# Expert rows of a mixture-of-experts layer padded to 128 instead of 256, with two blocks of separate experts in a slot

## What is computed

```python
def _L0_ffn_ref(x, Wg, bg, W1, b1, W2, b2):      # 4096 rows, D 256, FF 1024, 8 experts, top 2
    gate_logits = xt @ Wg + bg
    gate_scores = jax.nn.softmax(gate_logits, axis=-1)
    topk_scores, topk_idx = jax.lax.top_k(gate_scores, TOP_K)
    topk_scores = topk_scores / jnp.sum(topk_scores, axis=-1, keepdims=True)
    combine = jnp.sum(jax.nn.one_hot(topk_idx, N_EXPERTS, dtype=xt.dtype) * topk_scores[..., None], axis=1)
    h = jax.nn.gelu(jnp.einsum('td,edf->etf', xt, W1) + b1[:, None, :], approximate=False)
    expert_out = jnp.einsum('etf,efd->etd', h, W2) + b2[:, None, :]
    out = jnp.einsum('te,etd->td', combine, expert_out)
...
x = x + _L0_gnn_ref(_layernorm(x, axis=-1), adj, L0_gnn_W, L0_gnn_b)
x = x + _L0_ffn_ref(_layernorm(x, axis=-1)[None], L0_ffn_Wg, ...)[0]
x = x + _L1_gnn_ref(_layernorm(x, axis=-1), adj, L1_gnn_W, L1_gnn_b)
x = x + _L1_ffn_ref(_layernorm(x, axis=-1)[None])[0]
```

## Time and profile before

| | |
|---|---|
| median of three runs | 1059.9 us (1057.33 to 1060.02) |
| span of the profiled execution | 1056.5 us |
| TensorE busy | 954.7 us (90%), 6711 matmuls |
| VectorE, ScalarE, GpSimd busy | 539.1, 403.2 and 359.3 us |
| first-layer matmuls of the experts | 1776, 201.6 us |
| second-layer matmuls of the experts | 1776, 199.9 us |
| gelu on ScalarE | 296, 124.0 us |
| gathers and scatters on GpSimd | 72 and 74, 71.6 and 122.2 us |

### The profile page before, as it was taken

How to read it: one execution, slowest core, us unless ns; L and a number is a source line. 1 busy time by engine, 2 the same in 40 slices (tenths; PEclk the granted TensorE clock), 3 DMA queues, 4 the chain that set the end, 5 groups by cost and what they waited for, 6 DMA issues and landing times. The chain is left out here.

```text
span 1056.5 us, 22251 instructions
## 1 busy us (share of the span) xinstructions
PE 954.7 (90%) x6711; PEld 625.2 (59%) x6712; DVE 539.1 (51%) x1602; ACT 403.2 (38%) x820; POOL 359.3 (34%) x414
## 2 busy tenths in 40 slices
PE   4988999999923899999999999999839999999994
PEld 1444544444511689889898888889714454444542
DVE  6744212218499665655656566565536333150644
ACT  4862767666787423233232323323102101010111
POOL 3410000014567244545455454554535320110110
PEclk9999999999965899999999999999969999999998
DMA  9885898899788432323323233232359978875781
GB/s 338 326 290 174 286 334 323 295 349 361 277 292 230 143 63 41 56 45 48 53 43 53 45 50 50 42 54 45 55 173 394 409 265 298 293 241 187 227 277 40
DMA packets 92079, 199.84 MB, mean 189 GB/s; under 512 B 14368, under 2 KB 47904, under 8 KB 91904
## 3 DMA queue, kind: packets, MB, share of 16 engines
q1 hardware_dynamic: 70304, 164.17, 44.4%
q0 software_dynamic: 17552, 30.88, 14.7%
q10 hardware_dynamic: 4176, 4.19, 1.2%
HBM read 176.54 MB, written 22.68 MB: 189 GB/s over the span
## 5 line engine op out<-in xcount | busy, mean ns | idle before, releaser
L962 PE MATMUL bank<-adj_f,feat 128*128 128x512 f16 x1024 | 241.2, 391 | 16.6 <-DMA adj_f<-in_adjT 14.9
L1230 ACT ACTIVATE act_f<-bank,b_sb 128x256 f32<-128x256 f32 x296 | 124.0, 470 | 275.5 <-PE bank L1167 275.5
L1167 PE MATMUL bank<-rT,experts 128*128 128x256 f16 x1776 | 201.6, 274 | 3.0 <-DVE rT L1255 3.0
L1179 PE MATMUL bank<-experts,act_h 128*128 x1776 | 199.9, 273 | 0.0
L1167 PEld LDWEIGHTS bank<-rT,experts 128*128 x1776 | 174.1, 98 | 24.6 <-issue 3.4
L1179 PEld LDWEIGHTS bank<-experts,act_h 128*128 128x128 f16 x1776 | 172.0, 98 | 19.5
L962 PEld LDWEIGHTS bank<-adj_f,feat 128*128 128x128 f16 x1024 | 97.7, 97 | 143.7 <-issue 18.7
L1611 PE MATMUL bank<-adj_g,feat 128*128 128x512 f16 x768 | 179.6, 387 | 0.7 <-POOL feat L1437 0.7
L846 ACT ACTIVATE spent<-adj_f 128x1024 f16<-128x1024 f32 x128 | 135.1, 1055 | 33.6 <-DMA adj_f<-in_adjT 28.3
L1097 POOL DMA_INDIRECT x_rows<-y,token x74 | 122.2, 1651 | 65.5 <-issue 56.9
L1611 PEld LDWEIGHTS bank<-adj_g,feat 128*128 128x128 f16 x768 | 73.8, 96 | 94.4 <-issue 1.2
(11 more groups left out here) (259 smaller groups left out, 930.1 us busy)
## 6 DMA issues: line engine op xcount, KB each, us to landing
adj_f<-in_adjT SPq DMA_DIRECT2D x128, 512.0 KB, 6.5
adj_g<-in_adjT SPq DMA_DIRECT2D x72, 512.0 KB, 6.0
adj_early<-in_adjT SPq DMA_DIRECT2D x24, 512.0 KB, 7.1
adj_g<-in_adjT SPq DMA_DIRECT2D x48, 256.0 KB, 3.2
unit_f<-in_W SPq DMA_DIRECT2D x16, 512.0 KB, 7.4
stage<-in_W SPq DMA_DIRECT2D x12, 512.0 KB, 6.4
x_ring<-in_x POOLq DMA_DIRECT2D x16, 256.0 KB, 7.2
x_rows<-agg SPq DMA_DIRECT2D x4, 1024.0 KB, 8.5
```

Of the source, the lines that this page charges most:

```text
L962: last = pe.matmul(mine(s)[ib * DC + c][:, :], feat0[:, j, h, c * P:(c + 1) * P], adj_0[j % RING][:, ib * HALF_SWEEP:(ib + 1) * HALF_SWEEP ...
L1167: last = pe.matmul(pb[2 + q][:, k * SLOT:(k + 1) * SLOT], w1_part(e * DC + (f // FQ * W2_UNIT0 + c), wh)[:, (f % FQ) * P:(f % FQ + 1) * P] ...
L1179: last = pe.matmul(pb[6 + r][:, 0:D], act_h[:, ah, f, r * P:(r + 1) * P], experts[:, ds(e * DC + (W2_UNIT0 + f // UH), 1), wh, (f % UH) * ...
L1230: last = a.activation(act_f[q][:, k, :], pb[2 + q][:, k * SLOT:(k + 1) * SLOT], ACT.Gelu, bias=b1_sb[:, ds(e * FC + (2 * q + k), 1)], scal ...
```

## The change

The rows of an expert are rounded up to 128. A slot is still 256 places, but these are two blocks of 128 that may belong to two experts, and `table` holds an expert number for each block (`TABLE` = 76 entries in place of 40). All that depends on the expert is done per block: TensorE's weights in the first layer (so its matmuls have 128 moving columns, 96 a slot) and in the second, gelu and its bias on ScalarE (4 instructions of 128 columns a quarter), the gate copy and the second bias on VectorE. `BLOCKS` goes from 80 to 72. The compare table `past` moves from PSUM into the space of `row_hot` in SBUF.

```diff
-MAX_SLOTS = (2 * T + E * (SLOT - 1)) // SLOT
-MAX_PAIRS = (MAX_SLOTS + 1) // 2
-BLOCKS = 2 * MAX_PAIRS * SR
+MAX_BLOCKS = (2 * T + E * (P - 1)) // P
+MAX_SLOTS = (MAX_BLOCKS + SR - 1) // SR
+BLOCKS = MAX_SLOTS * SR
+TABLE = BLOCKS + 2 * SR
...
-    past = pb[6][:, P:P + 2 * MAX_PAIRS * E].rearrange("p (s e) -> p s e", e=E)
+    past = row_hots[:, :, :, :].rearrange("p i q c -> p (i q c)")[:, 0:TABLE * E].rearrange("p (s e) -> p s e", e=E)
...
-            st.link(v.tensor_scalar(need_i, running[:, NT, :], float(SLOT - 1), None, ALU.add))
-            st.link(v.tensor_single_scalar(need_i, need_i, -SLOT, ALU.bitwise_and))
+            st.link(v.tensor_scalar(need_i, running[:, NT, :], float(P - 1), None, ALU.add))
+            st.link(v.tensor_single_scalar(need_i, need_i, -P, ALU.bitwise_and))
...
-            def expert_of(s):
-                return pe.value_load(table[0:1, ds(s, 1)], min_val=0, max_val=E - 1)
+            def experts_of(s):
+                return [pe.value_load(table[0:1, ds(s * SR + r, 1)], min_val=0, max_val=E - 1) for r in range(SR)]
...
                     f = 2 * q + k
-                    m = 0
-                    for c in range(DC):
-                        for wh, xh in ((0, 0), (0, 1), (1, 0)):
-                            last = pe.matmul(pb[2 + q][:, k * SLOT:(k + 1) * SLOT],
-                                             w1_part(e * DC + (f // FQ * W2_UNIT0 + c), wh)[:, (f % FQ) * P:(f % FQ + 1) * P],
-                                             rT[:, xh, c, :], start=(m == 0), stop=(m == 5))
-                            m += 1
+                    for r in range(SR):
+                        m = 0
+                        for c in range(DC):
+                            for wh, xh in ((0, 0), (0, 1), (1, 0)):
+                                last = pe.matmul(pb[2 + q][:, k * SLOT + r * P:k * SLOT + (r + 1) * P],
+                                                 w1_part(e[r] * DC + (f // FQ * W2_UNIT0 + c), wh)[:, (f % FQ) * P:(f % FQ + 1) * P],
+                                                 rT[:, xh, c, r * P:(r + 1) * P], start=(m == 0), stop=(m == 5))
+                                m += 1
...
                             last = pe.matmul(pb[6 + r][:, 0:D], act_h[:, ah, f, r * P:(r + 1) * P],
-                                             experts[:, ds(e * DC + (W2_UNIT0 + f // UH), 1), wh,
+                                             experts[:, ds(e[r] * DC + (W2_UNIT0 + f // UH), 1), wh,
...
-                e = a.value_load(table[0:1, ds(s, 1)], min_val=0, max_val=E - 1)
+                e = [a.value_load(table[0:1, ds(s * SR + r, 1)], min_val=0, max_val=E - 1) for r in range(SR)]
...
-                        last = a.activation(act_f[q][:, k, :], pb[2 + q][:, k * SLOT:(k + 1) * SLOT], ACT.Gelu,
-                                            bias=b1_sb[:, ds(e * FC + (2 * q + k), 1)], scale=1.0 / WS)
+                        for r in range(SR):
+                            last = a.activation(act_f[q][:, k, r * P:(r + 1) * P], pb[2 + q][:, k * SLOT + r * P:k * SLOT + (r + 1) * P],
+                                                ACT.Gelu, bias=b1_sb[:, ds(e[r] * FC + (2 * q + k), 1)], scale=1.0 / WS)
...
-                v.tensor_copy(gates[:, ds(s * SR, SR)], rows[:, :, ds(D + e, 1)].rearrange("p r a -> p (r a)")
-                              ).then_inc(sem("gates_taken"), 1)
+                for r in range(SR):
+                    last = v.tensor_copy(gates[:, ds(s * SR + r, 1)], rows[:, r, ds(D + e[r], 1)])
+                last.then_inc(sem("gates_taken"), 1)
...
-                                                  in1=b2_all[:, ds(e, 1), :].rearrange("p a d -> p (a d)"),
+                                                  in1=b2_all[:, ds(e[r], 1), :].rearrange("p a d -> p (a d)"),
```

More of the change, by code:

```diff
@@ L45 @@
 MIDDLE_RING = 4
-LAST_SLOT = 2 * MAX_PAIRS
+LAST_SLOT = TABLE
 ROW = D + E
@@ L117, in program @@
     spare = keep("spare", [P, 1], F32)
-    slots_i = keep("slots_i", [P, 2 * MAX_PAIRS], I32)
+    slots_i = keep("slots_i", [P, TABLE], I32)
     dg = keep("dg", [P, NT], F32)
@@ L133, in program @@
     tokens = keep("tokens", [P, BLOCKS + 4 * SR], I32)
-    gates = keep("gates", [P, BLOCKS], F32)
+    gates = keep("gates", [P, TABLE], F32)
     shift1 = gates[:, 0:NT]
-    table = keep("table", [P, 64], I32)
+    table = keep("table", [P, TABLE + 4], I32)
     grow = keep("grow", [P, P], F32)
@@ L240, in program @@
     w = Region(SUM_AT, SUMS_END)
-    row_hot = [w(f"row_hot{i}", [P, HOTS, P], F16) for i in range(2)]
+    row_hots = w("row_hots", [P, 2, HOTS, P], F16)
+    row_hot = [row_hots[:, i, :, :] for i in range(2)]
     blk_hot = [w(f"blk_hot{i}", [P, HOTS, BLOCKS], F16) for i in range(2)]
@@ L271, in program @@
     need = pb[7][:, (at := next(small)):at + E]
-    slots_f = pb[7][:, (at := next(small)):at + 2 * MAX_PAIRS]
+    slots_f = pb[7][:, (at := next(small)):at + TABLE]
     w1_v = w1_flat.rearrange("p (h a t) f -> p a t h f", h=2, t=2)
@@ L818, in _ @@
             st.link(v.tensor_copy(slots_f, slots_i[:, :]))
-            st.link(v.tensor_tensor(past, slots_f.unsqueeze(2).broadcast_to([P, 2 * MAX_PAIRS, E]),
-                                    end_at[:, :].unsqueeze(1).broadcast_to([P, 2 * MAX_PAIRS, E]), ALU.is_ge))
+            st.link(v.tensor_tensor(past, slots_f.unsqueeze(2).broadcast_to([P, TABLE, E]),
+                                    end_at[:, :].unsqueeze(1).broadcast_to([P, TABLE, E]), ALU.is_ge))
             st.link(v.tensor_reduce(slots_f, past, AX, ALU.add))
-            st.did(v.tensor_scalar(table[:, 0:2 * MAX_PAIRS], slots_f, float(E - 1), None, ALU.min))
+            st.did(v.tensor_scalar(table[:, 0:TABLE], slots_f, float(E - 1), None, ALU.min))
             st.link(v.tensor_scalar(table[:, LAST_SLOT:LAST_SLOT + 1], end_at[:, E - 1:E], -1.0, None, ALU.add))
@@ L1064, in _ @@
                 i, m = q // HOTS % 2, q % HOTS
-                pe.matmul(pb[2][:, 0:BLOCKS], row_hot[i][:, m, :], blk_hot[i][:, m, :], start=(q == 0), stop=(q == 2 * NT - 1)
+                pe.matmul(pb[2][:, 0:BLOCKS], row_hots[:, i, m, :], blk_hot[i][:, m, :], start=(q == 0), stop=(q == 2 * NT - 1)
                           ).then_inc(sem("inverse_used"), 1)
@@ L1192, in _ @@
             keep_busy(pe, pb[1], 8)
-            e = expert_of(0)
+            e = experts_of(0)
             pe.wait_ge(sem("rT_ready"), 1)
@@ L1239, in _, with experts_of @@
             v.sem_inc(sem("y_scaled"), SR)
+            def experts_of(s):
+                return [v.value_load(table[0:1, ds(s * SR + r, 1)], min_val=0, max_val=E - 1) for r in range(SR)]
             def split_hidden(s, q):
@@ L1263, in take_y @@
             def take_y(s):
-                e = v.value_load(table[0:1, ds(s, 1)], min_val=0, max_val=E - 1)
+                e = experts_of(s)
                 v.wait_ge(sem("act_h_used"), (s + 2) * FQ)
```

14 lines of the change are left out of this document (7 added, 7 removed).

## The result

The changed kernel takes **1236.9 us** (median; 1235.6 to 1237.5), the kernel before 1058.6 us beside it on the same chip: a ratio of 1.168, with a 95% interval of 1.1655 to 1.1705. The forecast was 1223 us in a range of 1190 to 1262. The direction, the mechanism and its place were right. The time is 14 us above the forecast, and most of that comes from one short stretch, the head of the loop.

A forecast was written before the change was run, and what follows sets the result against it. TensorE's array bounds the kernel now; after the change its sequencer would, at 17.0 us a slot. Loop +167.5, first pass -2.0, first slot +1.5, GpSimd -4.0, routing +0.3: +163 on 1059.9, 1223 us, range 1190 to 1262.

The forecast's parts named there:

- first slot's own first layer: Ahead of the loop: 4.2 us more of TensorE's sequencer, partly hidden in a wait for VectorE; 0 to 3, taken +1.5.
- 34 slots: Expert layer's slot loop: rows rounded to 128 give 68 blocks, 34 slots for 37; three passes of 10.93 us go.
- The array's side: TensorE's first layer: 96 matmuls of 128 columns at 56 ns, 5.4 us for 5.24; a slot of 11.1 us.
- The rival with weight loads in the open: TensorE's first layer: weight loads of 98 ns set the pace, a slot of 15.1 us, 1165 us; chance 3%.
- the one in which the steps are free: Slot loop: register steps cost nothing beside matmuls, the array sets 11.1 us a slot, 1033 us; chance 4%.
- First layer 8.7 us, second 4.4, transposes and two loads 1.9: TensorE's sequencer per slot: 64 and 32 register steps at about 0.13 us, plus additions, transposes and number loads.
- The loop's head: Start of each pass on TensorE's sequencer: loop end and expert number 1.3 us, one more load 0.7, so 2.0.
- The GpSimd tail: Kernel's end: GpSimd, behind before, keeps up in a longer period; 4 us taken off (between 0 and 6).
- "1.5 us to spare": Kernel before, slot loop: the sequencer needs 9.4 us against the array's 10.93, so it is hidden with 1.5 us to spare.
- "The queue between them can't help": Changed slot loop: the queue between sequencer and array hides nothing, as the sequencer (17.0 us) is behind in every slot.
- The rival at 1368 us: Slot loop: TensorE's clock falls for good as the array works 11.1 of 17 us; a slot 21.4 us; chance 7%.
- ScalarE's and VectorE's additions: Slot loop: four gelus a quarter for two, a second gate copy (0.17 us) and extra loads fit idle time, no cost.

The follow-up runs named there:

- act_wide: Changed kernel with ScalarE as in the kernel before (one expert number a slot, 256-column gelus): 1234.9 us, ratio 1.1671 to the kernel before.
- dve_one_load: Changed kernel with VectorE loading one expert number a slot in the place of two: 1236.9 us, ratio 1.1689 to the kernel before.
- dve_load_moved: Changed kernel with VectorE's two number loads for its y step made two splits earlier: 1238.4 us, ratio 1.1696 to the kernel before.

## Why the prediction was right, and where it was off

The sum of the forecast was +163 us; the spans differ by 179.2. Its terms against the trace, by the first matmul of each stage (the first slot starts at 351.35 before and 350.89 after; the second first layer at 359.97 and 361.93; the last second layer at 757.49 and 936.30; the next stage's matmuls at 787.18 and 964.81):

| term | forecast | measured |
|---|---|---|
| routing, up to the first slot | +0.3 | -0.5 |
| first slot's own first layer | +1.5 | +2.4 |
| loop | +165.5 | +176.9 |
| behind the loop | -4.0 | -1.2 |
| the last stage | 0 | +1.6 |
| sum | +163.3 | +179.2 |

- **34 slots** for 37: right.
- **The array's side**, 56 ns for a narrow matmul with its weight load: right (5.36 us for 96). The rival with weight loads in the open is excluded for this kernel, as is the one in which the steps are free.
- **First layer 8.7 us, second 4.4, transposes and two loads 1.9**: 8.7, 4.4, 1.85. A step cost mostly 0.124 to 0.15 us as before, with one matmul behind it as with four. This was the heart of the forecast.
- **The loop's head**: the mis-sized term. "Loop end and expert number 1.3" and "two more loads 0.7 each" gave 2.0 here, and it takes 2.4. A load of a number was priced once, by a load in a quiet place; the new first one falls behind a scatter, and takes 0.3 us more in nearly every pass. The other 0.1 is 1.34 us for the 1.3 and 0.75 for the 0.7. 33 passes by 0.37 us are 12 us, three quarters of what is missing.
- **The GpSimd tail**: I took off 4.0 us since GpSimd would keep up. It does, in the loop; but the last two scatters of either kernel are made one behind the other at its end, and 1.2 us were gained. The last stage's 1.6 us I can't explain.
- **"1.5 us to spare"** in the kernel before: wrong as a statement, though no term rested on it. It set sums against each other, where the queue carries at most 1.9 us from one phase to the next. Spare were 0.5. "The queue between them can't help" was right, for the changed kernel.
- **The clock**: was at its upper level (1.00 in the stretch shown) but for five dips of 3.4 us, with gaps of 1.2 to 1.3 us ahead of each layer. The first dip is in the loop's first pass. The passes with the other four take 17.35 to 17.40 us, no longer than their neighbours: the array has time to spare. The rival at 1368 us didn't come about.

```profile
485.60:489.00 3.40, 3.40 (x35) 3.26 (x33) 0.38 (x2) 1.23 (x5) 1.59 (x1) 0.51 0.11 8
```

- **ScalarE's and VectorE's additions** at no cost: right for ScalarE (act_wide) and for VectorE's loads (dve_one_load, dve_load_moved).

## What to carry to other kernels

A register step or a load that makes an address is work of the issuing engine, and here it has a price of its own, 0.13 us and 0.75 us, which doesn't shrink with the matmul behind it. Before making tiles finer, count the steps of one pass in the compiled order and set them against the array's time: phase by phase and not as a sum, since the lead that the sequencer can save up is about 17 matmuls, half as long in time when they are half as wide. Where only a few tiles need the finer form, a branch that leaves the others on the coarse path costs less than the form itself (here 17.4 us a slot became 11.0).

## What the runs showed of the hardware that I hadn't expected

- TensorE's sequencer runs ahead of the array by about 17 load-and-matmul pairs: 1.9 us at 256 columns; 0.98 us at 128; two periods worked out with it agree within 0.05 us (13.1 for 13.11, 15.3 for 15.35). The Trainium skill (TensorE: Matmul & The Clock Gate, Back-to-back issue gap) speaks of a 64-deep window; 17 pairs are 34 instructions, about half of that.
- A load of one number into a register takes 300 ns, and 420 to 650 where it falls 0.65 to 0.95 us behind the end of a scatter instruction of GpSimd (139 loads in five kernels; one in a sixth took 320). A load of two numbers takes 540.
- 96 load-and-matmul pairs of 128 columns in a row went at 56 ns each, though a weight load is recorded at 95 to 98 ns there.
